# Scale rows kept in one PSUM bank and read there by VectorE's maxima; rows of softmax sums in one bank

## The reference, cut to what matters

```
f  = b[:, :, ::2, ::2]                    # 64 channels, 40 x 40
w  = 3x3 patches of f                     # 1600 patches, 576 values each
wn = w / max(norm(w), 1e-4)
yi = einsum('bpd,bld->blp', w, wn) * mm   # scores: patch l against place p
yi = softmax(10 * yi, axis=1) * mm        # over l
patches = einsum('blp,bld->bpd', yi, raw 4x4 patches of b)
out = patches overlap-added at stride 2, / 4
```

## Time and profile before

| | us |
|---|---|
| median of 3 runs | 1367.72 (1367.48 to 1370.94) |
| profiled execution, its own time | 1372.19 |
| span of its instructions | 1370.4 |
| DVE busy | 1169.1 (85%), 2315 instructions |
| ACT busy | 994.5 (73%), 2881 |
| POOL busy | 584.3 (43%), 510 |

### The profile page before, as it was taken

How to read it: one execution, slowest core, us unless ns; L and a number is a source line. 1 busy time by engine, 2 the same in 40 slices (tenths; PEclk the granted TensorE clock), 3 DMA queues, 4 the chain that set the end, 5 groups by cost and what they waited for, 6 DMA issues and landing times.

```text
span 1370.4 us, 20011 instructions
## 1 busy us (share of the span) xinstructions
PE 1194.4 (87%) x4910; PEld 750.1 (55%) x4910; DVE 1169.1 (85%) x2315; ACT 994.5 (73%) x2881; POOL 584.3 (43%) x510
## 2 busy tenths in 40 slices
PE   4785988979888889989899899988899889897896
PEld 3555654656546655565556555566555655465443
DVE  4576999889998899879998899988998799988872
ACT  2888676886778868796768877787777967687331
POOL 1002543346442554336442464425643365334772
PEclk9887999999999999999999999999999999999898
DMA  5311344335353353443444353533534434432442
GB/s 80 44 36 46 100 120 110 89 94 138 89 128 87 99 129 97 115 104 100 124 107 98 96 137 96 126 84 97 137 91 114 111 94 115 106 85 83 136 141 55
DMA packets 179175, 138.36 MB, mean 101 GB/s; under 512 B 119602, under 2 KB 177010, under 8 KB 179058
## 3 DMA queue, kind: packets, MB, share of 16 engines
q1 hardware_dynamic: 178898, 136.57, 39.2%
q10 hardware_dynamic: 160, 0.50, 0.2%
HBM read 19.76 MB, written 13.11 MB: 24 GB/s over the span
## 4 chain that ended last, share of the span: by engine, by line
DVE 43%; PE 21%; issue 17%; ACT 14%; SPq 2%; DMA 2%; DVEq 1%; POOL 1%; ACTq 0%; POOLq 0%
PE psO L586 12%; DVE S L1039 10%; DVE G L1102 9%; DVE Z L1126 8%; PE psG L534 6%; DVE G L999 6%; ACT S L808 5%; DVE G L994 3%; ACT G L727 2%; ACT G L819 2%; PE psG L549 1%; DVE Z L1123 1%; DVE Z L1122 1%; DMA SH<-G 1%; SPq L388 1%
## 5 line engine op out<-in xcount | busy, mean ns | idle before, releaser
L1243 POOL TENSOR_TENSOR G<-G,SH 123x492 f32<-123x492 f32 (+1 forms) x448 | 548.1, 1232 | 768.9 <-DMA SH<-G 766.3
L586 PE MATMUL psO<-Z,B 123*128 123x492 f32 (+2 forms) x1792 | 720.8, 533 | 73.8 <-DVE Z L1126 61.0
L586 PEld LDWEIGHTS psO<-Z,B 123*128 123x128 f32 x1792 | 336.3, 195 | 291.1 <-issue 142.1
L1039 DVE CUSTOM_DVE_ANT_0 S<-G,RB 123x492 f32<-123x492 f32 (+1 forms) x448 | 346.1, 784 | 18.5 <-ACT G L727 18.1
L819 ACT ACTIVATE G<-G,nb 123x492 f32<-123x492 f32 (+1 forms) x448 | 268.3, 642 | 128.5 <-DVE G L1102 126.9
L808 ACT ACTIVATE S<-S,nm 123x480 f32<-123x480 f32 (+3 forms) x560 | 309.1, 554 | 7.1
L534 PE MATMUL psG<-LH,HL 128*123 128x492 f16 (+2 forms) x1104 | 275.9, 359 | 32.0 <-ACT G L727 20.8
L1102 DVE SCALAR_TENSOR_TENSOR G<-G,RA,psB 123x492 f32<-123x492 f32 (+1 forms) x448 | 269.8, 644 | 0.4 <-PE psB L469 0.4
L1126 DVE TENSOR_TENSOR Z<-G 123x984 f32<-123x984 f32 (+2 forms) x192 | 230.5, 1200 | 29.3 <-POOL G L1243 27.6
L534 PEld LDWEIGHTS psG<-LH,HL 128*123 128x123 f16 x1104 | 144.4, 138 | 147.0 <-issue 64.8
L534 PE MATMUL psG<-H 128*123 128x492 f16 (+2 forms) x368 | 130.3, 354 | 0.0
(11 more groups left out here) (85 smaller groups left out, 748.0 us busy)
## 6 DMA issues: line engine op xcount, KB each, us to landing
SH<-G SPq DMA_DIRECT2D x336, 214.8 KB
SH<-G SPq DMA_DIRECT2D x112, 89.2 KB
SH<-G SPq DMA_DIRECT2D x336, 19.2 KB
XP<-x SPq DMA_DIRECT2D x20, 280.0 KB, 4.2
XP<-mid SPq DMA_DIRECT2D x20, 280.0 KB, 4.1
HL<-LH SPq DMA_DIRECT2D x16, 246.5 KB, 3.7
mid<-OSB SPq DMA_DIRECT2D x48, 80.0 KB, 2.4
out<-OSB SPq DMA_DIRECT2D x48, 80.0 KB, 2.3
```

Of the source, the lines that this page charges most:

```text
L586: last = pe.matmul(psO[:, b, 0:n], B[:, o:o + 128], Z[:, 2 * (s % 2) + j, 0:n], start=t == 0, stop=t == TILES - 1)
L1039: dve.tensor_tensor_reduce(S[:, slot, 0:n], G[:, g:g + n], RB[:, s0 * TW:s0 * TW + n], 1.0, 0.0, ALU.mult, ALU.max, mx[:, slot:slot + 1]). ...
L1243: pool.tensor_tensor(g, g, SH[:, o % SFREE, 0:n], ALU.add).then_inc(y1_made, 1)
```

## The change

- `RB`, `R`, the four ACT copies of a unit and `ROW_BANK` are gone. `psB` (two banks) becomes `psL` (rows of softmax sums) and `psR` (scale rows), one bank each.
- PE spreads the scale row of score chunk k (2, 4, 4, 4 tiles, out of `RA`) into `psR` at the chunk's first pair, j = 7k, behind that pair's `second_half`, hence at steps 2, 9, 16 and 22. It first waits until all maxima of the chunk before are done. DVE's first maxima of every chunk wait for that row.
- The maxima read `psR` as their first input and `G` as their second.
- So that the bank comes free, the odd maxima of pairs 6, 13 and 20 are made in their own step, as those of 22 and 27 were before (`AT_ONCE`).
- `lse_row` spreads into the one bank `psL`: chunk 0 at step 24 as before, chunks 1, 2 and 3 at the ends of steps 2, 9 and 16, each after all arguments of the chunk before.

```diff
+AT_ONCE = [6, 13, 20, 22, 27]
...
-        RB = sb("RB", [TW, TILES * TW], F32)
...
-        psB = ps("psB", [128, 2, 512])
+        psL = ps("psL", [128, 512])
+        psR = ps("psR", [128, 512])
...
-            def scale_rows(u, v, g):
+            def scale_rows(v, k):
 
                 pe.wait_ge(r_step, (v + 1) * R_STEPS)
-                if u is not None:
+                if v or k:
                     pe.sem_inc(pe_gate, 1)
-                    if g == 2:
-                        pe.wait_ge(b_made, (u + 1) * PAIRS)
-                    else:
-                        pe.wait_ge(arg_made, u * NB + (3 if g == 3 else NK) * TILES)
-                if g == 1:
+                    pe.wait_ge(max_made, v * NB + k * TILES)
+                s0, n = S_CHUNKS[k]
+                spread(psR[0:TW, :], RA, v * TILES + s0, v * TILES + s0 + n).then_inc(r_rows, 1)
+
+            def lse_row(v, k):
+
+                pe.wait_ge(lse_dve, v * LSE_STEPS + (LSE_STEPS // 2 if k == 0 else LSE_STEPS))
+                if v or k:
                     pe.sem_inc(pe_gate, 1)
-                    pe.wait_ge(r_rows, v * 4 + 1)
-                spread(ROW_BANK[g], R, 4 * g, min(4 * g + 4, TILES)).then_inc(r_psum, 1)
...
+                    pe.wait_ge(arg_made, v * NB + k * TILES)
                 s0, n = P_CHUNKS[k]
-                spread(psB[0:TW, k % 2, :], lse, s0, s0 + n).then_inc(lse_rows, 1)
+                spread(psL[0:TW, :], lse, s0, s0 + n).then_inc(lse_rows, 1)
...   (body of PE)
+                    if pairs and pairs[0] % PAIRS == 0:
+                        scale_rows(v, pairs[0] // PAIRS)
...
-                        lse_row(v, w, 0)
-                    if s == FIRST and u is not None:
-                        lse_row(u, v, 1)
+                        lse_row(v, 0)
+                    if u is not None and s % PAIRS == FIRST and s // PAIRS < NK - 1:
+                        lse_row(u, s // PAIRS + 1)
...   (ACT)
-            def scale_rows(v, g):
-                act.wait_ge(r_psum, v * 4 + g + 1)
-                n = min(4, TILES - 4 * g) * TW
-                act.activation(RB[:, 4 * g * TW:4 * g * TW + n], ROW_BANK[g][:, 0:n], ACT.Copy).then_inc(r_rows, 1)
...   (DVE, maxima)
-                if i == 0 and par == 0 and k != 1:
-                    dve.wait_ge(r_rows, v * 4 + max(k + 1, 2))
+                if i == 0 and par == 0:
+                    dve.wait_ge(r_rows, v * NK + k + 1)
                     dve.sem_inc(dve_gate, 1)
...
-                dve.tensor_tensor_reduce(S[:, slot, 0:n], G[:, g:g + n], RB[:, s0 * TW:s0 * TW + n], 1.0, 0.0,
+                dve.tensor_tensor_reduce(S[:, slot, 0:n], psR[0:TW, 0:n], G[:, g:g + n], 1.0, 0.0,
                                          ALU.mult, ALU.max, mx[:, slot:slot + 1]).then_inc(max_made, 1)
...   (DVE, score_pair)
-                if j - 1 not in (-1, 22):
+                if j and j - 1 not in AT_ONCE:
                     maxima(v, j - 1, 1)
                 next(adds, None)
                 next(adds, None)
                 maxima(v, j, 0)
-                if j in (22, SLOTS - 1):
-
+                if j in AT_ONCE:
                     maxima(v, j, 1)
...   (DVE, arguments)
-                                             in1=psB[0:TW, k % 2, 0:n],
+                                             in1=psL[0:TW, 0:n],
```

More of the change, by code:

```diff
@@ L174, in contextual_attention @@
         rcp = sb("rcp", [TW, TILES], F32)
-        R = sb("R", [TW, TILES], F32)
         RA = sb("RA", [TW, UNITS * TILES], F32)
@@ L212, in contextual_attention @@
         norm_cols = sem("norm_cols")
-        r_psum = sem("r_psum")
         blk_psum = sem("blk_psum")
@@ L243, in contextual_attention @@
         stored = sem("stored")
-        R_STEPS = 10
+        R_STEPS = 9
         LSE_STEPS = 12
@@ L253, in contextual_attention @@
         N_F = 4
-        ROW_BANK = [psB[0:TW, 1, :], psB[0:TW, 1, :], psM[0:TW, :], psB[0:TW, 0, :]]
         def p_cols(k):
@@ L453, in row_squares @@
                 pe.sem_inc(pe_gate, 1)
-                if v is not None:
-                    pe.wait_ge(r_rows, v * 4 + 3)
+                if v:
+                    pe.wait_ge(b_made, v * PAIRS)
                 for r in range(FROWS // 2):
@@ L471, in spread @@
                 return last
-            def scale_rows(u, v, g):
+            def scale_rows(v, k):
                 pe.wait_ge(r_step, (v + 1) * R_STEPS)
-                if u is not None:
+                if v or k:
                     pe.sem_inc(pe_gate, 1)
-                    if g == 2:
-                        pe.wait_ge(b_made, (u + 1) * PAIRS)
-                    else:
-                        pe.wait_ge(arg_made, u * NB + (3 if g == 3 else NK) * TILES)
-                if g == 1:
-                    pe.sem_inc(pe_gate, 1)
-                    pe.wait_ge(r_rows, v * 4 + 1)
-                spread(ROW_BANK[g], R, 4 * g, min(4 * g + 4, TILES)).then_inc(r_psum, 1)
[L487 to L496, removed]
+                    pe.wait_ge(max_made, v * NB + k * TILES)
[4 more added lines that the diff above has]
+                if v or k:
+                    pe.sem_inc(pe_gate, 1)
+                    pe.wait_ge(arg_made, v * NB + k * TILES)
                 s0, n = P_CHUNKS[k]
-                spread(psB[0:TW, k % 2, :], lse, s0, s0 + n).then_inc(lse_rows, 1)
+                spread(psL[0:TW, :], lse, s0, s0 + n).then_inc(lse_rows, 1)
             def block_group(v, w, g):
@@ L508, in block_group @@
                     pe.wait_ge(r_step, w * R_STEPS + 4)
-                else:
-                    pe.wait_ge(r_rows, v * 4 + 3)
+                elif v:
+                    pe.wait_ge(b_made, v * PAIRS)
                 for t in (2 * g, 2 * g + 1):
@@ L594, in body @@
                     pairs = score_list(s) if v is not None else []
[L595 to L602, removed]
                     if s == FIRST and v is not None:
@@ L634, in body @@
                         block_group(v, w, s - 21)
-                    if w is not None and s in (25, 26):
-                        scale_rows(u, w, s - 25)
             pe.wait_ge(mask_step, 2)
@@ L651, in _ @@
             band_sums(None, 0)
-            scale_rows(None, 0, 0)
-            scale_rows(None, 0, 1)
             body(None, 0, 1)
@@ L878, in body @@
                         softmax_pair(at)
[L879 to L882, removed]
                     if w is not None:
@@ L889, in body @@
                             roots(w)
-                        if s in (25, 26):
-                            scale_rows(w, s - 25)
                     if v is not None and (NK - 1) * PAIRS <= s < SLOTS - 1:
@@ L905, in _ @@
             roots(0)
-            scale_rows(0, 0)
-            scale_rows(0, 1)
             act.wait_ge(mask_ready, 1)
@@ L947, in squared_norms, with scales @@
                 dve.tensor_scalar(nsq[:, :], psM[0:TW, 0:TILES], 1e-8, None, ALU.max).then_inc(r_step, 1)
-            def scales(v, w):
+            def scales(w):
                 at = w * R_STEPS
@@ L959, in scales @@
                 dve.wait_ge(r_step, at + 8)
-                if v is not None:
-                    dve.sem_inc(dve_gate, 1)
-                    dve.wait_ge(r_rows, (v + 1) * 4)
                 mm = mm20[:, bass.ds(w * TILES, TILES)]
-                dve.tensor_tensor(R[:, :], rcp[:, :], mm, ALU.mult).then_inc(r_step, 1)
                 dve.tensor_tensor(RA[:, bass.ds(w * TILES, TILES)], rcp[:, :], mm, ALU.mult).then_inc(r_step, 1)
@@ L1164, in body @@
                         if s == 20:
-                            scales(v, w)
+                            scales(w)
             dve.wait_ge(mask_step, 1)
@@ L1206, in _ @@
             squared_norms(0)
-            scales(None, 0)
+            scales(0)
             body(None, 0, 1)
```

## The result

The changed kernel takes 1305.11 us (median of 4 runs, 1304.12 to 1310.59) against 1369.33 (1367.48 to 1372.62) for the kernel before: a ratio of 0.9537, 95% interval 0.9503 to 0.9571. Faster was forecast, but 1349 us with a range from 1325: the gain is 64 us, not 20.

What follows compares the result with a forecast made beforehand. It took neither PE nor DVE alone as the bound, with POOL's adds stopping DVE's maxima. 1372.2 - 35 - 4 + 8.4 + 7 + 2 + 2.5 = 1353, less 4.5 is 1349 us; range 1325 to 1376.

Steps and rivals of the forecast that it cites:

- Part 1: Maxima read PSUM and G instead of two SBUF inputs: 35 us off the time, bounds 0 and 61.
- The standing still: DVE's maxima with both inputs in SBUF stop while POOL's add reads SBUF: 81.6 us excess over the span.
- stage 2: Second stretch of an overlapping body, called PE's (33.03 busy of 34.00 us); no gain counted there.
- stage 4: Fourth stretch of an overlapping body, called PE's (31.91 of 33.76 us); 0.6 of 2.8 us gain counted.
- The sum at the bounds: All edits taken at their bounds, said to give 1315 and 1400 us.
- The chain's share: Second estimate of the maxima's gain: 24% of L1039's time is excess; 24% of its 137 us on the chain is 32.
- Parts 2 to 6: ACT copies gone, 4 us less; added: step 9 8.4, step 16 7, steps 2 and 22 2, first and last body 2.5.
- part 6: First and last body pass the same places once between them: 2.5 us cost, bounds 0 and 6.
- POOL still stops the maxima: Rival: G as second input still shares POOL's path, so the maxima gain nothing: 1384 us, chance 0.13.
- PE takes over: Rival: half of DVE's win is handed back waiting for PE, leaving 19 us: 1365 us, chance 0.17.
- More than that goes: Rival: the maxima's gain is 61 us: 1323 us, chance 0.12.
- The clock: Smaller rival within the forecast: step 16's new wait brings another lower-clock PE stretch per body, 8 us: 1357 us.

Runs made afterwards that it cites:

- e2: Changed kernel with ACT copying each scale row to SBUF and the maxima reading that copy and G, both in SBUF: 1408.55 us (1.0326).
- e1: Changed kernel with ACT copying each scale row into an SBUF tile, the maxima still reading the PSUM bank: 1324.33 us (0.9706).
- e10: Changed kernel plus ACT's scale-row copies, only score chunk 0's maxima (pairs 0 to 6) reading the SBUF copy: 1353.44 us (0.9896).
- e15: Changed kernel with a 16-column DVE copy and a wait ahead of each of score chunk 0's 112 maxima: 1320.07 us (0.9664).
- e16: Changed kernel with a 16-column DVE copy and a wait ahead of each of score chunk 3's 112 maxima: 1318.66 us (0.9654).
- e6: Changed kernel with POOL's adds of the shifted copy cut to their first 2 columns: 1256.10 us (0.9204).
- e5: Kernel before with POOL's adds of the shifted copy cut to their first 2 columns: 1261.48 us (0.9240).
- e14: Changed kernel with score chunk 1's scale row spread ahead of second_half of pair 7, not behind it: 1299.93 us (0.9509).
- e7: Kernel before with only the single bank for softmax-sum rows, spread at the ends of steps 2, 9 and 16: ratio 1.0018.
- e11: Kernel before with only the odd maxima of pairs 6, 13 and 20 moved into their own step: 1384.17 us (1.0137).
- e4: Changed kernel with the maxima's two inputs in the order G, scale row: 1306.42 us (0.9565).

## Why the prediction was wrong, step by step

*Part 1, the failed step.* The standing still was right in each of its numbers: 664 ns out of PSUM, no fixed cost beside SBUF's, 82 us of excess gone (81.6 forecast), DVE busy down by 80.2 ("some 80"). L999 and `Z` did not take it over: 98.7 + 230.5 us before, 91.3 + 241.2 after as L965 and L1091. What failed is the factor to the end of the kernel. The forecast let 35 of 82 through, "where DVE sets the pace", and cut each stage's gain at the time that PE had free. Shown instead: e2 less e1, 84.2 us for 92.7; e10, 26 for 32, most of it in stages 2 and 3; e15, 15.1 for 17.4 to 21, mostly in stage 2; e16, 13.7 for 20.9 where nothing was counted. PE's busy time in stage 2 was not a floor: more DVE time made the stage longer and PE's busy time with it (e10, e15). For stage 4 no run shows it as clearly. Over the whole body PE had 146.45 us of 159.49, and has 144.35 of 152.72 after. How DVE's time gets through such a stage, by late inputs of PE or by PE's clock, is not shown.

The forecast's own rule was also used one-sidedly: it charged stage 4 with 0.65 us for six more transposes of the spreads and gave stage 2, which it called PE's, nothing for the six that left it.

The sum at the bounds was wrong too. The stated bounds give 1372.2 - 61 - 8 + 4.2 + 2.1 - 4.5 = 1305 and 1372.2 + 17.5 + 20.3 + 5 + 6 - 4.5 = 1416.5, not 1315 and 1400. That the measured 1305 is the lower of the two is chance: part 1 went beyond its 61, and the costs were not at their lowest.

*The chain's share, used as a cross-check,* gave 32 and seemed to confirm 35. A chain charges time to DVE only while it runs through DVE; that it ran elsewhere through PE's work which DVE had delayed before is an explanation, not shown. Both readings are of one profile, and the shares of 81.6 us that they let through, 35 and 32, fall short in the same way of what the runs show.

*Parts 2 to 6, the costs.* Forecast 20 us, less 4 for ACT's copies. If the 82.5 us of excess came through at e2's nine tenths, 75 us, and the kernel gained 64, what is left is 11 us for the new waits, order and banks less the copies: an estimate by difference, and 16 was forecast. Without POOL's adds the same parts gained 5 us (e6 against e5), so it is a loose one. Its parts: the start, where part 6 put a cost, gained some 5 us, by ACT's copies that are gone (e1). At step 9 the maximum starts 3.80 us after the step's `Z`, where it had 1.99 (514.15 and 512.16), so 1.8 us later, not 1.4: the forecast took the four transposes at 0.59 us, and PE was at the lower clock level. Over the kernel DVE waits 18.4 us for scale rows and 2.2 for sums' rows, together at the top of the "8 to 20"; e14 takes 5 us off the time. At step 16 PE waits 1.17 us:

```profile
525.72 0.69 PE L471 MATMUL psR<-idn,RA 123*123 123x123 f32 x4 [1.17 <-DVE mx L1005]
```

1.5 was forecast, and over the kernel PE waits for maxima eight times, 11.6 us. The sums' bank costs 2.5 us (e7). The order of the odd maxima was priced at 4 us; alone, out of SBUF, it costs 16 (e11), in part as contention, and what it costs in the change no run tells.

*The rivals.* "POOL still stops the maxima" fell with the maxima's 664 ns and with e4: it does not matter which input is in PSUM. The Trainium skill's rule in "SBUF — State Buffer", section "Who interferes with whom", on an instruction with at most one SBUF input holds in this order too. "PE takes over" fell with e15. "More than that goes", given 0.12, was the right side, and still short: it let three quarters of the excess through.

*The clock* stood in the forecast as a possible loss of 8 us. The mean granted clock went the other way, 0.966 to 0.974, and PE's busy time for the same 4910 records fell by 18 us. How much of the gain that is, no run separates. That the clock follows DVE's time is shown by e1 and e2, which differ in the maxima's inputs alone (0.974 and 0.960).

## What to carry to other kernels

Where two engines feed each other within a step, a stage in which one is busy for 95% need not be bounded by it: compare its busy time over the whole repeated body (here 146 of 159 us) with the body's length. Count its instructions per stage and ask which of them the change itself moves. A mean duration that does not follow the columns can be worth most of its excess (here nine tenths, e1 and e2), also in stages in which the other engine looks full; price it by one run with a dummy load of that size before believing a chain's share. An edit that only shifts instructions can change what they lose to contention (e11), so its price in one kernel need not hold in the other.

## What the runs showed of the hardware that was not expected

- Taking POOL's adds away gives the kernel before 104 us (e5), more than the change: the change frees the maxima alone, and the other DVE instructions with two SBUF inputs still stand behind POOL (L965 over 246 columns 628 ns after, 413 in e6).
- Which of the two inputs is in PSUM makes 4 ns of difference (660 and 664, e4), and there is no standing still either way: the longest of 448 maxima is 673 ns in the changed kernel and 669 in e4, 1705 before.
- Moving three odd maxima a unit from the next step into their own, with both inputs in SBUF, changes what the maxima lose to POOL by 15 us (e11).
